# Graph layers on one core: SyncE copies the rows of 48 gather columns, GpSimd gathers 48 columns fewer

## The chip, the cores and the metric

The kernel runs on one core of a Trainium2 chip. The metric is the device time of one execution in microseconds (us). Engines are named as in the profile: PE (TensorE), DVE (VectorE), ACT (ScalarE), POOL (GpSimd), SP (SyncE). A name with a q behind it (SPq, DVEq) is the sequencer of that engine: what it issues or signals, not what it computes.

## What is computed

Four graph layers run one after the other over 6,250 nodes with 128 features and 206,250 directed edges, given as two lists, src and dst; dst is sorted. Between them stand a layer norm, a ReLU and a residual sum. Cut to what matters here:

```
h = relu(layernorm(x))
# layer 0: attention over src, sum over dst
scores = sum(query * key);  alpha = softmax of the edges with the same src
out = segment_sum(msg * alpha * count, dst);  two dense layers with batch norm
# layer 1: softmax over dst, 8 heads, with a bias from the edge features
agg = segment_sum(softmax(q[dst] . k[src] + edge @ We) * v[src], dst);  agg @ Wo
# layer 2: softmax over dst, 4 heads
out = segment_sum(softmax(leaky(e_src[src] + e_dst[dst])) * h[src], dst)
# layer 3: weighted sum over dst
agg = segment_sum(edge_weight * x[src], dst);  two dense layers, leaky relu
```

All weights, the features and the row numbers come in as float32 and int32; the output is [6250, 128] float32.

## The kernel before, in words

The edges stand in 128 partitions of T = 1612 each. A layer over the edges is a *pass*. There are five: PB goes by source (the softmax of layer 0), and PA, P1, P2 and P3 go by destination (layers 0, 1, 2, 3). A pass takes its 1612 columns in 124 halves of K = 13 columns; two halves (b = 0 and 1, each with buffers of its own) are a pair, so that a pass has 62 pairs. What one half asks of each engine:

- **POOL** (`pass_pool`, L1369 to L1383) waits for `free{b}` and issues 13 indirect DMAs (L1382). One gathers a column: for each of 128 partitions the row of a node table that the row number in `ix_s` names. Rows are 264 floats wide in PA (table `qm0`), 256 in P1 (`kv1`), 132 in P2 (`h2`), 128 in P3 (`x3`).
- **DVE** (`pass_dve`) waits for `rows{b}`, multiplies the gathered rows by the rows of the other end (L1458), reduces (L1462), does the small softmax steps, lays the next half's near rows by a scan (`hold_rows`, L1430), weights (L1517, L1521 or L1513), frees the buffer (`leave`) and scans the half (L1528).
- **ACT** (`pass_act`) takes its steps in a fixed order, half by half: the start of the next near rows (L1557, L1559), the exponentials (L1600, L1603, L1563), the copy of near rows from `rows_d` (`near_rows_act`, L1546), and then, once the half is scanned, the carried column (L1621) and the rows of state for the store (L1622, L1624). Then it signals `laid{b}`.
- **SP** (`pass_sp`, L1661) has two DMAs per half, in P1 three: the load of near rows for the pair that follows (`near_load`, L1659), in P1 the edge bias (`bias_load`, L1654), and the store of the half's state (`pass_store`, L1650), which waits for `laid{b}`.

The order of SP is written out by hand in `two` and has no loop at run time. Its core:

```
for b in range(2):
    if not last and q.near is not None:
        sp.wait_ge(*q.on("made", i * 6 + (3 * b + 1)))
        near_load(sp, q, i + 1, b)
    ...
    pass_store(sp, q, i, b)
```

So the near load that a half needs is issued by SP behind the store of the half before it, and ACT cannot reach the state rows of a half (L1621, L1622) before it has copied the near rows (L1546). P3 has no near rows: there SP has only its store.

Of the kernel before, what the change touches and what calls it, by code (L numbers as in the profile page):

```python
# [19 lines left out]
I32 = mybir.dt.int32  # L20
# [6 lines left out]
P = 128  # L27
# [7 lines left out]
T = 1612  # L35
EP = P * T
K = 13
IT = T // K
assert EP >= E and T % (2 * K) == 0
PADN = 6271  # L40
# [55 lines left out]
def graph_layers_kernel(nc, A, out):  # L96
    with ExitStack() as ctx:
        def sb(name, shape, dt=F32):
            return ctx.enter_context(nc.sbuf_tensor(name, shape, dt))
# [18 lines left out]
        def dram(name, shape, dt=F32):  # L118
            return nc.dram_tensor(name, shape, dt).ap()
# [12 lines left out]
        ident = sb("ident", [P, P])  # L132
# [30 lines left out]
        head_i = [sb(f"head_i{o}", [P, 1], I32) for o in range(2)]  # L163
        patch_i = [sb(f"patch_i{o}", [P, 1], I32) for o in range(2)]
        head = sb("head", [P, D])

        bias2 = [sb(f"bias2_{o}", [P, P]) for o in range(2)]
        contT = [sb(f"contT{o}", [P, P]) for o in range(2)]
# [128 lines left out]
        psrow_src = [stat[:, :, :, :].rearrange("p j a h -> p (j a h)")[:, b * K * 12:(b + 1) * K * 12] for b in range(2)]  # L297


        keys_dram = dram("keys_in", [2, P, C])  # L300
        sorted_dram = dram("keys_sorted", [2, P * C])
        pay_dram = dram("payload", [EP, PW])
# [6 lines left out]
        h2_t = dram("h2", [NN * P, D + 4])  # L309
        ed2_t = dram("ed2", [NN * P, 4])  # L310
        x3_t = dram("x3", [NN * P, D])
        keyrow_t = [dram(f"keyrow{o}", [P, T], I16) for o in range(2)]

        qxb_t = dram("start_rows_by_src", [EP + NPAD, D])
# [5 lines left out]
        class Pass:  # L320
# [12 lines left out]

            def own(self, what):
                return S(f"{self.name}_{what}")

            def total(self, what):

# [22 lines left out]
        P2 = Pass("p2", H2, 32, True, h2_t, ed2_t, edx_t, 136)  # L361
        P3 = Pass("p3", 1, D, False, x3_t, None, None, D)
        passes = [PB, PA, P1, P2, P3]
        for q in passes:
            q.bv, q.abig, q.st, q.psrow, q.zt, q.prod = bv, abig, st, psrow, zt, prod
# [998 lines left out]
        def gathered_rows(q):  # L1364

            return rows_3 if q is P3 else rows_s

        def pass_pool(g_, q):
            wd_s = q.tabs.shape[1]  # L1369
            to = gathered_rows(q)  # L1370
            for nm in q.needs:
                g_.wait_ge(S(nm[0]), nm[1])
            if q.near is not None:
                g_.indirect_dma_start(head[:, 0:q.HF], None, q.tabd, bass.IndirectOffsetOnAxis(ap=head_i[q.o][:, 0:1], axis=0)).then_inc(q.s("head_in"), 16)
            with g_.Fori(0, IT // 2) as i:
                for b in range(2):
                    g_.wait_ge(*q.on(f"free{b}", i + 1))
                    if q is P1:
                        g_.wait_ge(q.own(f"next{b}"), i + 1)
                    g_.sem_inc(S("pool_go"), 1)  # L1380
                    for k in range(K):
                        g_.indirect_dma_start(to[b][:, k, 0:wd_s], None, q.tabs, bass.IndirectOffsetOnAxis(ap=ix_s[b][:, k:k + 1], axis=0))\  # L1382
                          .then_inc(q.own(f"rows{b}"), 16)  # L1383

        def heads(t, q):
            return t[:, 0:q.H, :]
# [22 lines left out]
        def pass_dve(v, q):  # L1409
# [22 lines left out]
            def half(i, b, last):  # L1432
# [225 lines left out]
        def near_load(sp, q, i, b):  # L1658
            sp.dma_start(rows_d[b][:, :, :].rearrange("p t w -> p (t w)")[:, 0:K * q.HF],  # L1659
                         q.near[0:EP, :].rearrange("(p t) w -> p (t w)", t=T)[:, bass.ds(i * (2 * K * q.HF) + b * K * q.HF, K * q.HF)]).then_inc(q.s(f"near_in{b}"), 16)  # L1660

        def pass_sp(sp, q):
            for b in range(2):
                sp.sem_inc(q.s(f"sent{b}"), 16)
            if q.near is not None:
                for nm in q.started:
                    sp.wait_ge(S(nm[0]), nm[1])
            for b in range(2):
                if q.near is not None:
                    near_load(sp, q, 0, b)  # L1670
                if q is P1:
                    bias_load(sp, 0, b)

            def two(i, last):
                if q is PB:
                    zeros_chunk_sp(sp, i)
                for b in range(2):
                    if not last and q.near is not None:
                        sp.wait_ge(*q.on("made", i * 6 + (3 * b + 1)))
                        near_load(sp, q, i + 1, b)  # L1680
                    if not last and q is P1:
                        sp.wait_ge(S(f"bias_used{b}"), i + 1)
                        bias_load(sp, i + 1, b)
                    if q is PB and not b and i + 2 < NPAY:
                        payload_in(sp, i + 2)
                    if q is PB and b and i:
                        payload_out(sp, i - 1)
                    pass_store(sp, q, i, b)
                if q is PB and last:
                    payload_out(sp, i)  # L1690

            if q is PB:
                payload_in(sp, 0)
                payload_in(sp, 1)
            peeled = 2 if q is PB else 1
            for i in range(IT // 2 - peeled):
                two(i, False)
            for i in range(IT // 2 - peeled, IT // 2):
                two(i, i == IT // 2 - 1)
# [476 lines left out]
        @block.vector  # L2176
        def _(v):
            padding_dve(v)
            keys_dve(v)
            sort_dve(v, 0)  # L2180
            with v.If(unsorted(v) > 0):
                sort_dve(v, 1)
                again_dve(v)
            src_dve(v)
            pass_dve(v, PB)
            carry_dve(v, PB)
            bias_dve(v, b2_0)
# [5 lines left out]
            v.sem_inc(S("edges_ready"), 1)  # L2193
            pass_dve(v, PA)
# [12 lines left out]
            end3_dve(v)  # L2207

        @block.scalar
        def _(act):  # L2210
            norm0_act(act)
            weights3_act(act)
            dst_act(act, 0)
            proj0_sort_act(act)
            with act.If(unsorted(act) > 0):
                for lp in range(1, LOGP + 1):
                    sort_act(act, 1, lp)
                again_act(act)
# [4 lines left out]
            carry_act(act, PB)  # L2223
            pass_act(act, PA)
# [12 lines left out]
        @block.tensor  # L2237
        def _(pe):
            flag_pe(pe)
            weights3_pe(pe)  # L2240
            dst_pe(pe, 0)
            proj0_sort_pe(pe)
            with pe.If(unsorted(pe) > 0):
                for lp in range(1, LOGP + 1):
                    sort_pe(pe, 1, lp)
                dst_pe(pe, 1)
            src_pe(pe)
            payload_pe(pe)
            carry_pe(pe, PB)
            carry_pe(pe, PA)  # L2250
# [32 lines left out]
```

## Time and profile before

| | |
|---|---|
| median of 3 runs | 11,406.7 us (11,404.31 to 11,411.17) |
| profiled execution, its own time | 11,410.4 us |
| its span, first to last instruction | 11,408.5 us |
| busy: POOL, DVE, ACT, PE | 8,190.2, 7,216.0, 5,413.3, 956.1 us |
| chain that ended last | POOL 61%, issue 24%, DVE 7%, DMA 4% |

The passes take most of the span: PB from 644 to 2,660 us, PA from 2,798 to 4,836, P1 from 5,010 to 7,026, P2 from 7,183 to 9,199, P3 from 9,297 to 11,313. Between them stand the dense parts and the patches. The busy time of POOL is that of its indirect DMAs, one after the other; "issue" in the chain is the time between two of them in which POOL waited for nothing that the profile shows. A row of SPq is an issue: how long SP's sequencer was taken up by one DMA. When the bytes land is given apart, as "us to landing", counted from the issue.

### The profile page before, as it was taken

What the parts mean: (1) busy time and instruction counts of PE and PEld (TensorE: products, weight loads), DVE (VectorE), ACT (ScalarE), POOL (GpSimd) and SP (SyncE); (2) the same over time, 40 slices, a digit from 0 to 9 for tenths busy, and PEclk for the clock granted to TensorE, in tenths of its full rate; (3) what the DMA queues carried; (4) which work ended last, traced back from release to release, by engine and by line L of the source; (5) the groups of instructions that cost most, each with busy time, mean ns of one, the idle gap of its engine ahead of it and who ended that gap; (6) DMA issues with size and microseconds to landing.
All of it is one profiled execution on the core that took longest, in us unless ns stands there. A gap on an engine that the chain in (4) does not pass through costs nothing.

```text
span 11408.5 us, 38369 instructions
## 1 busy us (share of the span) xinstructions
PE 956.1 (8%) x3312; PEld 677.7 (6%) x3312; DVE 7216.0 (63%) x6971; ACT 5413.3 (47%) x6326; POOL 8190.2 (72%) x8632
## 2 busy tenths in 40 slices
PE   4122222221000000030000001100000000000001
PEld 3111111110000000010000000000000000000001
DVE  8845555553888888869999997454444543333334
ACT  6244444442666666546766765333333333333332
POOL 2177777777777777667777776777777767777776
PEclk8555565555555555565555555555555555555555
DMA  8756666663666666546666665333333333333333
GB/s 307 275 193 204 202 206 200 204 202 109 215 211 216 210 216 211 198 148 224 223 222 226 220 226 160 96 110 113 110 113 111 112 96 103 107 103 106 106 104 97
DMA packets 792030, 1943.01 MB, mean 170 GB/s; under 512 B 214034, under 2 KB 425962, under 8 KB 791369
## 3 DMA queue, kind: packets, MB, share of 16 engines
q1 hardware_dynamic: 459776, 1126.04, 28.0%
q0 software_dynamic: 331904, 814.65, 24.9%
q14 instruction: 178, 1.45, 0.0%
q8 instruction: 28, 0.46, 0.0%
q10 hardware_dynamic: 144, 0.41, 0.0%
HBM read 1201.70 MB, written 738.73 MB: 170 GB/s over the span
## 4 chain that ended last, share of the span: by engine, by line
POOL 61%; issue 24%; DVE 7%; DMA 4%; ACT 2%; PE 1%; POOLq 0%; SPq 0%; DVEq 0%; ACTq 0%
POOL region L1382 58%; DMA region<-x,ix_s 2%; DVE psR L1513 2%; POOL work L1808 1%; DVE region L656 1%; DVE region L657 1%; DVE psB L1430 1%; DVE work L1528 1%; DVE psR L1521 0%; ACT work L1622 0%; POOL start_rows_by_dst L1136 0%; POOL start_ed L972 0%; DMA region<-h,ix_s 0%; POOL start_rows_by_src L1131 0%; PE psR L759 0%
## 5 line engine op out<-in xcount | busy, mean ns | idle before, releaser
L1528 DVE TENSOR_TENSOR_SCAN work<-work,psR 128x1792 f32<-128x1792 f32 (+2 forms) x496 | 1971.3, 3974 | 92.5 <-DVE ix_s L1449 56.5
L1382 POOL DMA_INDIRECT region<-x,ix_s x1612 | 1521.2, 944 | 502.3 <-issue 460.7
L1382 POOL DMA_INDIRECT region<-qm,ix_s x1612 | 1524.0, 945 | 492.6 <-issue 490.1
L1382 POOL DMA_INDIRECT region<-kv,ix_s x1612 | 1524.1, 945 | 491.0 <-issue 484.3
L1382 POOL DMA_INDIRECT region<-k,ix_s x1612 | 1521.5, 944 | 491.2 <-issue 490.9
L1382 POOL DMA_INDIRECT region<-h,ix_s x1612 | 1521.4, 944 | 491.2 <-issue 488.8
L1546 ACT COPY work<-region 128x1664 f32<-128x1664 f32 (+1 forms) x496 | 1162.2, 2343 | 1307.2 <-DMA region<-start_rows_by_dst 775.4
L1430 DVE TENSOR_TENSOR_SCAN psB<-psB,work 128x1792 f32<-128x1792 f32 (+1 forms) x496 | 1485.1, 2994 | 397.8 <-ACT psB L1559 350.8
L1622 ACT COPY work<-work 128x1664 f32<-128x1664 f32 (+2 forms) x496 | 1539.2, 3103 | 0.0
L1621 ACT COPY psR<-work 128x128 f32<-128x128 f32 (+2 forms) x496 | 189.3, 382 | 2463.9 <-DVEq L1529 2463.9
L1458 DVE TENSOR_TENSOR work<-region,psB 128x1664 f32<-128x1664 f32 x372 | 702.1, 1887 | 808.9 <-DMA region<-k,ix_s 528.2
L1513 DVE TENSOR_TENSOR psR<-region,psB 128x1664 f32<-128x1664 f32 x124 | 235.1, 1896 | 1244.9 <-DMA region<-x,ix_s 1244.9
L1559 ACT ACTIVATE psB<-restart 128x1792 f32<-128x1792 bf16 (+1 forms) x496 | 647.4, 1305 | 15.6
L1521 DVE TENSOR_TENSOR psR<-region,psR 128x1664 f32<-128x1664 f32 x248 | 467.0, 1883 | 212.5 <-ACT work L1600 212.5
L1476 DVE TENSOR_TENSOR s_max<-region,psB 128x52 f32<-128x52 f32 x124 | 30.4, 245 | 743.1 <-DMA region<-h,ix_s 743.1
L1462 DVE TENSOR_REDUCE psR<-work 128x52 f32<-128x1664 f32 (+1 forms) x248 | 469.9, 1895 | 8.6
L1600 ACT ACTIVATE work<-dd 128x56 f32<-128x56 f32 (+2 forms) x372 | 463.0, 1245 | 0.0
L1563 ACT ACTIVATE work<-restart 128x1792 f32<-128x1792 bf16 x248 | 417.8, 1685 | 0.3
L1281 PE MATMUL psR<-work,we_wide 128*128 128x384 f32 x620 | 327.9, 705 | 870.4 <-ACT work L1303 870.4
L1770 PE MATMUL psR<-cst,contT 128*128 128x128 f32 x4 | 1.6, 501 | 4261.0 <-DVEq L1731 4261.0
L1773 PE MATMUL psB<-work,ones 128*128 128x512 f32 x6 | 5.9, 1114 | 4057.7 <-DVEq L1709 4057.7
L1557 ACT COPY work<-psB 128x128 f32<-128x128 f32 (+1 forms) x492 | 156.9, 319 | 382.2 <-DVE s_max L1476 317.5
(339 smaller groups left out, 5050.9 us busy)
## 6 DMA issues: line engine op xcount, KB each, us to landing
region<-start_rows_by_dst SPq DMA_DIRECT2D x248, 832.0 KB, 6.8
state_p<-work SPq DMA_DIRECT2D x124, 936.0 KB, 4.9
state_p<-work SPq DMA_DIRECT2D x124, 884.0 KB, 3.8
region<-start_rows_by_src SPq DMA_DIRECT2D x124, 832.0 KB, 9.9
start_rows_by_dst<-zero_t SPq DMA_DIRECT2D x62, 1664.0 KB, 7.7
state_pA<-work SPq DMA_DIRECT2D x124, 832.0 KB, 4.9
state_p<-work SPq DMA_DIRECT2D x124, 832.0 KB, 3.5
start_rows_by_src<-zero_t SPq DMA_DIRECT2D x1, 59904.0 KB, 163.6
```

What stands on the lines that cost most here:

```text
L1382: g_.indirect_dma_start(to[b][:, k, 0:wd_s], None, q.tabs, bass.IndirectOffsetOnAxis(ap=ix_s[b][:, k:k + 1], axis=0))\
L1430: nc.vector.tensor_tensor_scan(near_ps[:, 0:m], near_ps[:, 0:m], q.zt[:, 0:m], 0.0, ALU.mult, ALU.add).then_inc(q.s("held"), 1)
L1458: nc.vector.tensor_tensor(q.prod, rs[:, :, 0:D], hv[:, :, 1:K + 1].rearrange("p f t -> p t f"), ALU.mult).then_inc(q.s("dotted"), 1)
L1462: c.did(nc.vector.tensor_reduce(s.rearrange("p h t -> p t h"), q.prod.rearrange("p t (h d) -> p t h d", h=H), AX.X, ALU.add))
L1513: c.did(nc.vector.tensor_tensor(bvv[:, :, 1:K + 1].rearrange("p f t -> p t f"), rs[:, :, 0:D], w.unsqueeze(2).to_broadcast([P, K, D]), ALU ...
L1521: c.did(nc.vector.tensor_tensor(bvh[:, :, 0:dh, 1:K + 1].rearrange("p h j t -> p t h j"), rs[:, :, off:off + D].rearrange("p t (h j) -> p ...
L1528: c.do(nc.vector.tensor_tensor_scan(q.st[:, 0:F * (K + 1)], decay_at(q, b)[:, 0:F * (K + 1)], summed[:, 0:F * (K + 1)], 0.0, ALU.mult, ALU ...
L1546: nc.scalar.copy(f_by_t(q.zt, q.HF)[:, :, 1:K + 1].rearrange("p f t -> p t f"), rows_d[b][:, :, :].rearrange("p t w -> p (t w)")[:, 0:K * ...
L1559: nc.scalar.activation(f_by_t(near_ps, q.HF), restart[q.o][:, bass.ds(n, 1), :].to_broadcast([P, q.HF, K + 1]), ACT.Exp).then_inc(q.s("mad ...
L1563: return nc.scalar.activation(f_by_t(decay_at(q, b), q.F), restart[q.o][:, bass.ds(n, 1), :].to_broadcast([P, q.F, K + 1]), ACT.Exp)
L1600: nc.scalar.activation(f_by_t(decay_at(q, b), F).rearrange("p (h j) t -> p h j t", h=H), heads(dd, q).unsqueeze(2).to_broadcast([P, H, dh ...
L1622: ins = nc.scalar.copy(pr[:, :, 0:F], stv[:, :, 1:K + 1].rearrange("p f t -> p t f"))
```

## The change

In each of the four passes by destination (PA, P1, P2, P3), column 12 of half b = 1 is no longer gathered by POOL in one pair out of five: pairs 6, 11, 16, ... 61. These are 12 columns in a pass, 48 in all, one column in every ten halves. Their row numbers are the same in the four passes. They are brought once, ahead of PA: DVE copies the 12 columns of numbers (`numbers_dve`), PE turns them (`numbers_pe`), ACT copies them (`numbers_act`), and SP writes them to DRAM (`numbers_sp`). SP then waits for what the pass needs (its tables) before it starts on the pairs.

In pairs 0 to 59 of a pass, SP loads 25 or 26 of these numbers into its registers (`numbers_of`, one load instruction) and copies, for each, one row of the table to a DRAM buffer (`row_ahead`): 128 rows over five pairs, 25.6 per pair. These stand ahead of the near load of their half. Six pairs on, one DMA brings the 128 rows of the column into its place among the gathered rows (`column_in_sp`), and DVE waits for it too.

```
         def pass_sp(sp, q):
...
+            if q is AHEAD[0]:
+                numbers_sp(sp)
+            if q.ahead:
+                for nm in q.needs:
+                    sp.wait_ge(S(nm[0]), nm[1])
+
             def two(i, last):
                 if q is PB:
                     zeros_chunk_sp(sp, i)
+                j = i // PAIRS_AHEAD
+                fetch = q.ahead and j < COLS_AHEAD
+                if fetch:
+                    a, z = part_of(i)
+                    numbers = numbers_of(sp, j, a, z)
                 for b in range(2):
+                    if brought(q, i, 1) and not b:
+                        column_in_sp(sp, q, columns_ahead(i) - 1)
+                    if fetch:
+                        mid = (a + z) // 2
+                        for r in (range(a, mid), range(mid, z))[b]:
+                            row_ahead(sp, q, j, r, numbers[r - a])
                     if not last and q.near is not None:
                         sp.wait_ge(*q.on("made", i * 6 + (3 * b + 1)))
                         near_load(sp, q, i + 1, b)
```

The new functions that it calls:

```
+        def row_ahead(sp, q, j, r, number):
+
+            wd = q.tabs.shape[1]
+            sp.dma_start(ahead_t[j, r:r + 1, 0:wd], q.tabs[bass.ds(number, 1), :]).then_inc(S(f"row_ahead{column_number(q, j) % 2}"), 16)
...
+        def column_in_sp(sp, q, j):
+
+            wd = q.tabs.shape[1]
+            c = column_number(q, j)
+            sp.wait_ge(S(f"row_ahead{c % 2}"), (c // 2 + 1) * 16 * P)
+            sp.wait_ge(*q.on("free1", FIRST_AHEAD + j * PAIRS_AHEAD + 1))
+            sp.dma_start(gathered_rows(q)[1][:, K - 1, 0:wd], ahead_t[j, :, 0:wd]).then_inc(S("column_in"), 16)
```

On POOL (`pass_pool`) a half with such a column issues 12 gathers instead of 13, and on DVE (`pass_dve`) its first wait changes:

```
-                v.wait_ge(q.own(f"rows{b}"), i * (16 * K) + 16 * K)
+                v.wait_ge(*q.rows(b, gathered(q, i, b)))
+                if brought(q, i, b):
+                    v.wait_ge(S("column_in"), 16 * (column_number(q, columns_ahead(i) - 1) + 1))
```

**How instructions move on SP, PA, one half (b = 1 of the first pair).** Before, the near load stands right behind the store of the half ahead of it:

```order
L1659 DMA region<-start_rows_by_dst 128x1664 [waits pass_made]
L1650 DMA state_pA<-work 128x1664 [waits pass_laid0]
L1659 DMA region<-start_rows_by_dst 128x1664 [waits pass_made]
L1650 DMA state_pA<-work 128x1664 [waits pass_laid1]
L1659 DMA region<-start_rows_by_dst 128x1664 [waits pass_made]
```

In the changed kernel L1698 is the store, L1707 the near load, L1738 the load of numbers, and an ISA with a DMA at L1734 is one row copy (its address is worked out from the register, then the copy is issued). The same place starts so:

```order
L1698 DMA state_pA<-work 128x1664 [waits pass_laid0]
L1734 ISA
L1734 DMA rows_ahead<-qm 12x22
L1734 ISA
L1734 DMA rows_ahead<-qm 12x22
```

and ends so, with 13 such couples between store and near load:

```order
L1734 ISA
L1734 DMA rows_ahead<-qm 12x22
L1707 DMA region<-start_rows_by_dst 128x1664 [waits pass_made]
L1698 DMA state_pA<-work 128x1664 [waits pass_laid1]
L1738 TENSOR_LOAD numbers_ahead
```

Between a store and the near load that followed it at once there are now 12 or 13 row copies and, in every second half, the load of numbers too.

**On POOL, PA, the last pair of the changed loop's body of five.** Before, each half of the loop's body reads "one gather with a wait, then x12". Now the fifth half b = 1 has one less:

```order
L1406 DMA region<-qm,ix_s 128x264 [waits pass_free0]
L1406 DMA region<-qm,ix_s 128x264 x12
L1406 DMA region<-qm,ix_s 128x264 [waits pass_free1]
L1406 DMA region<-qm,ix_s 128x264 x11
```

Here L1406 is the gather that was L1382; nothing else moved on POOL.

## Rows read from the trace of the kernel before

**Rows 1.** The page: busy time of two engines, and the chain that ended last.

```profile
DVE  8845555553888888869999997454444543333334
POOL 2177777777777777667777776777777767777776
...
POOL 61%; issue 24%; DVE 7%; DMA 4%; ACT 2%; PE 1%; POOLq 0%; SPq 0%; DVEq 0%; ACTq 0%
```

**Rows 2.** Groups of instructions, line L1382 (busy us, mean ns, idle before us and releasers).

```profile
L1382 POOL DMA_INDIRECT region<-kv,ix_s x1612 | 1524.1, 945 | 491.0 <-issue 484.3 <-DVEq L1447 6.7
L1382 POOL DMA_INDIRECT region<-x,ix_s x1612 | 1521.2, 944 | 502.3 <-issue 460.7 <-DVEq L1451 30.2 <-DVE ix_s L1425 11.4
```

**Rows 3.** Timelines of SP and ACT in one half of PA (start, duration).

```profile
4008.47 0.32 SPq L1650 DMA_DIRECT2D state_pA<-work  x1
4008.83 0.43 SPq L1659 DMA_DIRECT2D region<-start_rows_by_dst  x1
4015.37 3.04 ACT L1546 COPY work<-region 128x1664 f32<-128x1664 f32 x1 [2.92 <-DMA region<-start_rows_by_dst]
4020.91 0.38 ACT L1621 COPY psR<-work 128x128 f32<-128x128 f32 x1 [2.49 <-DVEq L1529]
4024.33 0.32 SPq L1650 DMA_DIRECT2D state_pA<-work  x1
```

**Rows 4.** The same of one half of P1.

```profile
6201.97 0.32 SPq L1650 DMA_DIRECT2D state_p<-work  x1
6202.33 0.43 SPq L1659 DMA_DIRECT2D region<-start_rows_by_dst  x1
6209.81 3.04 ACT L1546 COPY work<-region 128x1664 f32<-128x1664 f32 x1 [3.39 <-DMA region<-start_rows_by_dst]
6214.18 0.17 ACT L1620 COPY psR<-m_ext 128x8 f32<-128x8 f32 x1 [1.32 <-DVEq L1529]
6218.19 0.32 SPq L1650 DMA_DIRECT2D state_p<-work  x1
```

**Rows 5.** The same of one half of P2.

```profile
8500.95 0.32 SPq L1650 DMA_DIRECT2D state_p<-work  x1
8501.32 0.43 SPq L1659 DMA_DIRECT2D region<-start_ed  x1
8511.71 0.39 ACT L1621 COPY psR<-work 128x132 f32<-128x132 f32 x1 [6.08 <-DVEq L1529]
8515.39 0.32 SPq L1650 DMA_DIRECT2D state_p<-work  x1
```

**Rows 6.** The same of one half of P3, which has no near load.

```profile
10523.74 0.38 ACT L1621 COPY psR<-work 128x128 f32<-128x128 f32 x1 [10.97 <-DVEq L1529]
```

**Rows 7.** The page, DMA issues: count, KB each, us from issue to landing.

```profile
region<-start_rows_by_dst SPq DMA_DIRECT2D x248, 832.0 KB, 6.8
state_pA<-work SPq DMA_DIRECT2D x124, 832.0 KB, 4.9
...
region<-start_ed SPq DMA_DIRECT2D x124, 26.0 KB, 3.6
```

**Rows 8.** Single lines on SP (duration ns min/median/max).

```profile
L587 SPq TENSOR_LOAD <-flag_i x4: 287/480/904, 490.2 to 4835.2; - x4
L587 SPq FUSED_REGOPS  x4: 154/158/192, 490.8 to 4835.6; - x4
L538 SPq DMA_DIRECT2D state_pA<-ctz x1: 252/252/252, 41.7 to 41.7; - x1
L494 SPq DMA_DIRECT2D we_wide<-in_L_gnn_We_dram x2: 532/564/597, 34.9 to 35.4; - x2
L494 SPq DMA_DIRECT2D be_col<-in_L_gnn_be_dram x1: 600/600/600, 36.1 to 36.1; - x1
L494 SPq DMA_DIRECT2D w3raw<-in_L_gnn_W_dram x2: 432/432/432, 39.0 to 40.4; - x2
```

More of the change, by code:

```diff
@@ L297, in graph_layers_kernel @@
         psrow_src = [stat[:, :, :, :].rearrange("p j a h -> p (j a h)")[:, b * K * 12:(b + 1) * K * 12] for b in range(2)]
+        PAIRS_AHEAD = 5
+        COLS_AHEAD = (IT // 2 - 2) // PAIRS_AHEAD
+        FIRST_AHEAD = PAIRS_AHEAD + 1
+        COL_AHEAD = FIRST_AHEAD * 2 * K + 2 * K - 1
+        assert 2 + PAIRS_AHEAD * COLS_AHEAD == IT // 2
         keys_dram = dram("keys_in", [2, P, C])
@@ L335, in own, with gathers, rows @@
                 return S(f"{self.name}_{what}")
+            def gathers(self, b):
+                return K * (IT // 2) - (COLS_AHEAD if self.ahead and b else 0)
+            def rows(self, b, value):
+                i = passes.index(self)
+                return S(f"rows{b}_{i % 3}"), value + sum(16 * q.gathers(b) for q in passes[i % 3:i:3])
             def total(self, what):
@@ L363, in graph_layers_kernel @@
         passes = [PB, PA, P1, P2, P3]
+        AHEAD = [PA, P1, P2, P3]
         for q in passes:
+            q.ahead = q in AHEAD
+            q.ahead_before = AHEAD.index(q) if q.ahead else 0
             q.bv, q.abig, q.st, q.psrow, q.zt, q.prod = bv, abig, st, psrow, zt, prod
@@ L1374, in pass_pool, with pair @@
                 g_.indirect_dma_start(head[:, 0:q.HF], None, q.tabd, bass.IndirectOffsetOnAxis(ap=head_i[q.o][:, 0:1], axis=0)).then_inc(q.s("head_in"), 16)
-            with g_.Fori(0, IT // 2) as i:
+            def pair(i, short):
                 for b in range(2):
@@ L1380, in pass_pool, with columns_ahead, brought, gathered @@
                     g_.sem_inc(S("pool_go"), 1)
-                    for k in range(K):
+                    for k in range(K - (short and b)):
                         g_.indirect_dma_start(to[b][:, k, 0:wd_s], None, q.tabs, bass.IndirectOffsetOnAxis(ap=ix_s[b][:, k:k + 1], axis=0))\
-                          .then_inc(q.own(f"rows{b}"), 16)
+                          .then_inc(q.rows(b, 0)[0], 16)
+            if q.ahead:
+                pair(0, False)
+                pair(1, False)
+                with g_.Fori(0, COLS_AHEAD) as j:
+                    for u in range(PAIRS_AHEAD):
+                        pair(j * PAIRS_AHEAD + (u + 2), u == PAIRS_AHEAD - 1)
+            else:
+                with g_.Fori(0, IT // 2) as i:
+                    pair(i, False)
+        def columns_ahead(i):
+            return max(0, (i - 1) // PAIRS_AHEAD)
+        def brought(q, i, b):
+            return q.ahead and b and i >= FIRST_AHEAD and (i - FIRST_AHEAD) % PAIRS_AHEAD == 0
+        def gathered(q, i, b):
+            return 16 * (K * (i + 1) - (columns_ahead(i) if q.ahead and b else 0))
         def heads(t, q):
@@ L1660, in near_load, with numbers_dve, numbers_pe, numbers_act @@
                          q.near[0:EP, :].rearrange("(p t) w -> p (t w)", t=T)[:, bass.ds(i * (2 * K * q.HF) + b * K * q.HF, K * q.HF)]).then_inc(q.s(f"near_in{b}"), 16)
+        def numbers_dve(v):
+            nc.vector.tensor_copy(numbers_f[:, :], oth_i[1][:, COL_AHEAD:T:2 * K * PAIRS_AHEAD]).then_inc(S("numbers"), 1)
+        def numbers_pe(pe):
+            pe.wait_ge(S("numbers"), 1)
+            nc.tensor.transpose(numbers_ps[0:COLS_AHEAD, :], numbers_f[:, :], ident[:, :]).then_inc(S("numbers"), 1)
+        def numbers_act(act):
+            act.wait_ge(S("numbers"), 2)
+            nc.scalar.copy(numbers_i[:, :], numbers_ps[0:COLS_AHEAD, :]).then_inc(S("numbers"), 1)
+        def numbers_sp(sp):
+            sp.wait_ge(S("numbers"), 3)
+            sp.dma_start(numbers_t, numbers_i[:, :]).then_inc(S("numbers"), 16)
+            sp.wait_ge(S("numbers"), 19)
+        def column_number(q, j):
+            return q.ahead_before * COLS_AHEAD + j
+        def row_ahead(sp, q, j, r, number):
+            wd = q.tabs.shape[1]
+            sp.dma_start(ahead_t[j, r:r + 1, 0:wd], q.tabs[bass.ds(number, 1), :]).then_inc(S(f"row_ahead{column_number(q, j) % 2}"), 16)
+        def numbers_of(sp, j, a, z):
+            return nc.values_load_multi_w_load_instructions(numbers_t[j:j + 1, a:z], engines=(mybir.EngineType.SP,), min_val=0, max_val=PADN,
+                                                            skip_runtime_bounds_check_because="a row number is the number of a node, at most PADN")[1]
+        def column_in_sp(sp, q, j):
[4 more added lines that the diff above has]
+            sp.dma_start(gathered_rows(q)[1][:, K - 1, 0:wd], ahead_t[j, :, 0:wd]).then_inc(S("column_in"), 16)
+        def part_of(i):
+            u = i % PAIRS_AHEAD
+            return P * u // PAIRS_AHEAD, P * (u + 1) // PAIRS_AHEAD
         def pass_sp(sp, q):
@@ L1672, in pass_sp @@
                     bias_load(sp, 0, b)
+            if q is AHEAD[0]:
+                numbers_sp(sp)
+            if q.ahead:
+                for nm in q.needs:
+                    sp.wait_ge(S(nm[0]), nm[1])
             def two(i, last):
```

8 lines of the change are left out of this document (added).

## The prediction
> **What bounds the kernel now.** I read the page first, for who is busy and what the chain of waits ends on. POOL is busy seven tenths in almost every slice, and POOL with its issue gaps is 85% of the chain [rows 1]. Then the gathers by pass: 1,612 of them, 945 ns each, with 0.30 us of issue gap between them and next to no wait for another engine; (1,524.1 + 491.0) / 1,612 = 1.25 us a column, 16.25 us a half of 13 columns and 32.5 us a pair, in all five passes [rows 2]. So POOL sets the pace, and a gather removed is worth at most 1.25 us.
>
> Then I asked who comes next, since a pass has three more engines with a fixed round per half. The timelines of PA and P1 show a second loop that is nearly as long. It runs through SP: ACT lays a half's state, SP issues the store and 0.36 us behind it the near load, the near rows land, ACT copies them (L1546), and only behind that, in ACT's own order, come L1621 and L1622, which lay the next half's state. The reader is to see in [rows 3, 4] that ACT stands idle for the near load (2.92 and 3.39 us), and that the slack of this loop is the wait of ACT that follows, for the scan: 2.49 us in PA, 1.32 us in P1. In P2 the near load is small and the slack is 6.08 us [rows 5]. P3 has no near load; its ACT waits 10.97 us a half for DVE [rows 6].
>
> **The gain.** 48 gathers go: 48 x 1.25 = 60 us, if POOL stays the bound. In a half without them DVE is not the limit in PA, P2 and P3 [rows 1]; in P1 it is nearly full, and perhaps 10 of the 60 stay there. So 50 to 60 us, 0.5% of the time.
>
> **What SP now issues.** Per pair, 25.6 row copies and one load of 25 or 26 numbers, in 60 of 62 pairs of each of the four passes: 6,144 copies, 240 loads. All stand between a store and the near load behind it, which is inside the loop above. Their price:
>
> - The address: one FUSED_REGOPS, 0.158 us [rows 8].
> - The copy's issue. SP's static copies take from 0.252 us (one row) to 0.432 us (128 rows). The built program marks nearly all of them as prepared ahead; two kinds in the weights' loads without that mark take 0.532 to 0.600 us [rows 8]. A copy whose address comes out of a register can't be prepared, so I take 0.56 us, the nearest rows. The ends are 0.25 us and, for what no row shows of register addresses, 0.87 us (0.56 plus twice the address step).
> - The step from one SP instruction to the next, 0.04 us (4008.47 + 0.32 to 4008.83) [rows 3], twice.
>
> That is 0.80 us a row (0.48 to 1.1) and 25.6 x 0.80 = 20.5 us a pair.
> - The load of numbers. A load of a single number takes 0.287 to 0.904 us, median 0.48 [rows 8]. For 25 the ends are 0.5 us (all at the price of one) and 25 x 0.287 = 7.2 us; nothing says which is nearer, and I take the middle, 3.8 us.
>
> Together S = 24.3 us a pair. The Trainium skill, page "Runtime: NRT & Kernel Launch", section "Instruction fetch mechanics", puts such a load at about 200 ns per register even in bulk; by that it would be an estimated 5.1 us a pair and the sum below 1.3 x 180 = 234 us more. No run here shows it yet.
>
> **The loop with S in it.** Per half, without waits:
>
> - PA: store to near load 0.36, copy 3.04, L1621 to the next store 3.42 (4020.91 to 4024.33), and the landing. Now 6.54 us pass from the issue (4008.83) until ACT has the rows (4015.37) [rows 3]. But behind a dozen row copies the near load no longer starts beside the 832 KB store; the store itself lands in 4.9 us with the load on its heels, against 6.8 for the load [rows 7]. I take 4.9 for the landing and keep 6.5 as the upper end. A half is 6.82 + 4.9 = 11.7 us, a pair 23.4 + 24.3 = 47.7 us against 32.5: 15.2 us x 60 pairs = **+912**.
> - P1: 0.36 + 3.04 + 4.01 (6214.18 to 6218.19) + 4.9 = 12.3 us; 7.48 us is the upper end of the landing [rows 4]. A pair is 24.6 + 24.3 = 48.9, so 16.4 x 60 = **+984**.
> - P2: 0.37 (8500.95 to 8501.32) + 3.6 for the landing [rows 7] + 0.26 for its short copy + 3.68 (8511.71 to 8515.39) [rows 5] = 7.9 us; a pair 15.8 + 24.3 = 40.1: 7.6 x 60 = **+456**. In P2 the slack of 6.08 us a half is eaten as well.
> - P3: SP needs 2 x 0.32 + 24.3 = 25 us of 32.5 a pair, and nothing is behind it but stores with two halves of room. It keeps its gain: **-15**.
>
> Sum: 912 + 984 + 456 - 15 = +2,337. Where the loop is the bound the removed gathers give nothing. The sum is against the profiled execution, 11,410.4 us (span 11,408.5 and 1.9 around it), 4 us above the median; on the median it gives about 13,750.
>
> **Small edits.** The copy of the numbers on DVE, the turn on PE, the copy on ACT and the write happen once, between PB and PA, by rows of 0.2 to 0.5 us and one DMA that lands like a small load, 3.6 us: under 10 us. SP's new wait for the tables delays only pair 0. The DMA that brings a column is one issue of about 0.43 us in 48 pairs, 20 us at most, and it is issued a half before DVE asks. What the copies move is 6,144 rows of about 1 KB, 6 MB of 1,943: no load for the DMA engines. On DVE the added wait finds its data there.
>
> **The rivals.** (a) *Faster*: the copies hide. The deciding point is what SP adds per half against the slack: 1.32 us in P1, 2.49 in PA, and up to 1.6 to 2.6 us more if the landing shortens. With 13 copies that is 0.2 to 0.35 us a row, all told. Then POOL stays the bound and the time is 11,406.7 - 55 = 11,350. For it speaks that SP has two short issues a half and idles 15 of 16 us; against it, that this idleness lies behind the store's wait and the copies stand in front of the near load, and that 0.158 + 0.252 + 0.08 = 0.49 us is the least the rows allow. The skill's page "DMA: Bandwidth & Descriptors", section "Issuing engines are not separate DMA queues", calls the sequencer's time to initiate a DMA usually small beside the DMA itself; by that rule this case would hold. [...]
>
> (b) *Slower, but little*: issues as short as prepared ones (0.49 us a row) and the numbers at the price of one. S = 25.6 x 0.49 + 0.5 = 13.0; PA 36.4 and P1 37.6 us a pair, +234 and +306, P2 28.8 us and hidden: 11,406.7 + 540 - 30 = 11,920.
>
> (c) *Much slower*: a register address costs more, 1.1 us a row, and the numbers 7.2 us. S = 35.4; pairs of 58.8, 60.0, 51.2 and 36.0 us: +1,578, +1,650, +1,122, +210, so about 15,970.
>
> (d) The column comes late and DVE waits for it. The rows are copied at least a pair before the DMA that collects them, so it would take a landing of over 16 us; it would add at most some us in 48 halves. It changes no sum.
>
> **How the numbers follow.** Two kernels differ measurably here from about 0.2%, 23 us. The forecast (slower through the near-load loop, S between 16 and 31 us) has 0.74, (b) and what lies below 16 us 0.11, (c) and beyond 0.10, (a) 0.04, no change 0.01. S = 16 gives 39.4, 40.6 and 31.8 us a pair, +414, +486 and nothing in P2, so about 12,280. S = 31 gives 54.4, 55.6, 46.8: +1,314, +1,386, +858, about 14,950. The range is these two, 12,280 to 14,950. Chances: faster 0.04, same 0.01, slower 0.95.
>
> **What the profile of the changed kernel would show.** The couples at L1734 at 0.80 us on SP, near loads issued 10 us and more behind their store; ACT idle before L1546 for the near load by some 10 us a half in PA and P1, and no wait any more at L1621 and L1620; POOL waiting at its first gather of a half, for DVE; PB and P3 as long as before, P3 shorter by 15 us; P1 the longest pass, P2 less stretched than PA. Near-load landings below 6.8 us. I would be wrong if ACT's wait at L1621 stays, if POOL still has only issue gaps in PA, or if the copies overlap their issue.

## The result and the profile after

The changed kernel takes 14,658.5 us (median of 4 runs, 14,653.0 to 14,667.3) against 11,408.8 us of the kernel before on the same chip: 1.285 times the time, 95% interval 1.2827 to 1.2872, or +3,250 us. The forecast was 13,750 with a range of 12,280 to 14,950: the right way, with a size 910 us short.

The page, in the lines that answer to [rows 1]:

```profile
DVE  8555555445444454555556556633333333433333
...
POOL 1477777644444444454444444465555555677776
...
SPq 34%; POOL 20%; issue 17%; DMA 13%; ACT 10%; DVE 5%; PE 1%; ACTq 0%; POOLq 0%; DVEq 0%
SPq L1734 23%; POOL region L1406 18%; SPq L1738 10%; DMA region<-start_rows_by_dst 8%; ACT work L1670 8%; DMA region<-start_ed 2%; DMA region<-x,ix_s 2%; DVE psR L1561 1%; POOL work L1917 1%; DVE region L679 1%; ACT psR L1669 1%; DVE region L680 1%; SPq L1698 1%; ACT work L1672 0%; DVE work L1576 0%
```

The slices are 367 us long. From the ninth on, just behind the start of PA, POOL is busy four to six tenths, and seven again only in the last ones, which are P3. SP's sequencer had 0% of the chain before; now it has 34%, and it names the row copies (L1734, 23%) and the loads of numbers (L1738, 10%). The gathers (source L1406, was L1382: ns min/median/max, first and last start) date the passes:

```profile
L1406 POOL DMA_INDIRECT region<-qm,ix_s x1600: 940/947/959, 2804.3 to 6206.8; - x178
L1406 POOL DMA_INDIRECT region<-kv,ix_s x1600: 940/947/1040, 6405.4 to 9524.2; - x178
L1406 POOL DMA_INDIRECT region<-h,ix_s x1600: 938/945/984, 9688.6 to 12467.9; - x178
L1406 POOL DMA_INDIRECT region<-x,ix_s x1600: 940/945/961, 12568.6 to 14566.0; - x178
```

A gather costs what it cost [rows 2]. First to last gather of a pass, in us (first and last starts in the traces), on chips on which the kernel before takes 11,407 to 11,409 us:

| | PA | P1 | P2 | P3 | the whole kernel |
|---|---|---|---|---|---|
| before | 2,014 | 2,014 | 2,011 | 2,011 | 11,409 |
| after | 3,403 | 3,119 | 2,779 | 1,997 | 14,659 |
| near load first (e1) | 2,303 | 2,248 | 2,097 | 1,996 | 12,008 |
| gathers back (e2) | 3,362 | 3,086 | 2,740 | 2,013 | 14,565 |
| numbers aligned (e3) | 3,115 | 2,793 | 2,457 | 1,996 | 13,726 |
| fixed rows, no numbers (e4) | 2,674 | 2,561 | 2,027 | 1,996 | 12,621 |
| near load first, aligned (e11) | 2,067 | 2,015 | 1,996 | 1,996 | 11,430 |

After minus before is +1,389, +1,105, +768 and -14, together 3,248 of the 3,250 us.

One half of PA, from a store to the next (timelines of SP and ACT after; L1698 store, L1734 copies, L1707 near load, L1594 near copy, L1669 and L1670 state rows), against [rows 3]:

```profile
3846.95 0.32 SPq L1698 DMA_DIRECT2D state_pA<-work  x1
3847.47 12.01 SPq L1734 DMA_DIRECT2D rows_ahead<-qm  x13
3859.52 0.50 SPq L1707 DMA_DIRECT2D region<-start_rows_by_dst  x1
3870.42 0.32 SPq L1698 DMA_DIRECT2D state_pA<-work  x1
```

```profile
3864.19 3.02 ACT L1594 COPY work<-region 128x1664 f32<-128x1664 f32 x1 [13.37 <-DMA region<-start_rows_by_dst]
3867.03 0.36 ACT L1669 COPY psR<-work 128x128 f32<-128x128 f32 x1
3867.32 3.04 ACT L1670 COPY work<-work 128x1664 f32<-128x1664 f32 x1
```

13 copies take 12.0 us; the near load goes out 12.6 us behind its store instead of 0.36, its rows are there 4.7 us later, and ACT runs straight through to the next store: 23.5 us instead of 15.9, with no wait left at L1669. The half after that holds a load of numbers too. Over the passes, two lines of the page say who waits: ACT for the near rows, 15.8 us a half in PA and P1 (3,849.6 us in 244 waits), and POOL in PA for DVE to free a buffer.

```profile
L1594 ACT COPY work<-region 128x1664 f32<-128x1664 f32 (+1 forms) x496 | 1159.5, 2338 | 6266.3 <-DMA region<-start_rows_by_dst 3849.6
L1406 POOL DMA_INDIRECT region<-qm,ix_s x1600 | 1514.0, 946 | 1891.5 <-DVEq L1497 1438.4
```

What SP pays (a copy of a row is cut into parts: 12 of 22 or 11 floats in PA and P2, 16 of 16 or 8 in P1 and P3; source views of L1734, L1738 and L1707, ns min/median/max; "us to landing" of the page), against [rows 7, 8]:

```profile
L1734 SPq FUSED_REGOPS  x6144: 37/37/48, 2810.7 to 14511.2; - x199
L1734 SPq MOVE rows_ahead<-qm x1536: 29/38/45, 2810.8 to 6155.3; - x192
L1734 SPq DMA_DIRECT2D rows_ahead<-qm x1536: 701/729/1325, 2810.9 to 6155.3; - x192
...
L1734 SPq DMA_DIRECT2D rows_ahead<-kv x1536: 492/492/1392, 6414.0 to 9472.8; - x192
...
L1734 SPq DMA_DIRECT2D rows_ahead<-h x1536: 701/724/1160, 9692.2 to 12425.0; - x192
```

```profile
L1738 SPq TENSOR_LOAD <-numbers_ahead x240: 2950/10690/12007, 2807.3 to 14482.5; - x120
```

```profile
region<-start_rows_by_dst SPq DMA_DIRECT2D x248, 832.0 KB, 5.0
...
region<-start_ed SPq DMA_DIRECT2D x124, 26.0 KB, 2.3
```

Within a half, copies start 0.924 us apart in PA (median; mean 0.944), 0.675 in P1 (mean 0.718), 0.918 in P2 (0.942). A load of 25 or 26 numbers takes 10.7 us in the median and 8.2 in the mean of PA, P1 and P2. With these the forecast's own loop gives, per pair: PA 2 x (6.82 + 5.0) + 24.2 + 8.2 = 56.0 us, P1 2 x (7.41 + 5.0) + 18.4 + 8.2 = 51.4, P2 2 x (0.37 + 2.3 + 0.26 + 3.68) + 24.1 + 8.1 = 45.4. Measured, as 32.5 + growth / 60: 55.6, 50.9 and 45.3 us.

### The profile page after: what moved, and what is told of

It reads as the page before. It is cut to its first block, busy times and chain, and to the rows that moved or that the text cites. A ratio compares the mean times of both kernels' runs of the same rounds, so it can differ in the third digit from the quotient of the medians.

```text
span 14665.2 us, 56702 instructions
## 1 busy us (share of the span) xinstructions
PE 956.2 (7%) x3313; PEld 678.2 (5%) x3313; DVE 7210.5 (49%) x6972; ACT 5339.6 (36%) x6327; POOL 8152.4 (56%) x8584
## 4 chain that ended last, share of the span: by engine, by line
SPq 34%; POOL 20%; issue 17%; DMA 13%; ACT 10%; DVE 5%; PE 1%; ACTq 0%; POOLq 0%; DVEq 0%
SPq L1734 23%; POOL region L1406 18%; SPq L1738 10%; DMA region<-start_rows_by_dst 8%; ACT work L1670 8%; DMA region<-start_ed 2%; DMA region<-x,ix_s 2%; DVE psR L1561 1%; POOL work L1917 1%; DVE region L679 1%; ACT psR L1669 1%; DVE region L680 1%; SPq L1698 1%; ACT work L1672 0%; DVE work L1576 0%
## 5 line engine op out<-in xcount | busy, mean ns | idle before, releaser
L1594 ACT COPY work<-region 128x1664 f32<-128x1664 f32 (+1 forms) x496 | 1159.5, 2338 | 6266.3 <-DMA region<-start_rows_by_dst 3849.6
L1406 POOL DMA_INDIRECT region<-qm,ix_s x1600 | 1514.0, 946 | 1891.5 <-DVEq L1497 1438.4
L1406 POOL DMA_INDIRECT region<-kv,ix_s x1600 | 1514.4, 946 | 1605.6 <-DVEq L1493 1154.2
L1406 POOL DMA_INDIRECT region<-h,ix_s x1600 | 1511.2, 945 | 1269.3 <-DVEq L1497 818.1
L1576 DVE TENSOR_TENSOR_SCAN work<-work,psR 128x1792 f32<-128x1792 f32 (+2 forms) x496 | 1971.3, 3974 | 92.0 <-DVE ix_s L1495 55.6
L1406 POOL DMA_INDIRECT region<-k,ix_s x1612 | 1522.8, 945 | 491.1 <-issue 490.8
L1406 POOL DMA_INDIRECT region<-x,ix_s x1600 | 1511.3, 945 | 498.7 <-issue 456.4
L1670 ACT COPY work<-work 128x1664 f32<-128x1664 f32 (+2 forms) x496 | 1536.9, 3099 | 0.0
L1669 ACT COPY psR<-work 128x128 f32<-128x128 f32 (+2 forms) x496 | 185.9, 375 | 1408.7 <-DVEq L1577 1389.2
L1542 DVE TENSOR_TENSOR_SCAN m_ext<-rst,psR 128x112 f32<-128x112 f32 (+1 forms) x248 | 81.5, 329 | 429.2 <-ACT work L1672 427.6
```

Of the source, the lines that this page charges most:

```text
L1576: c.do(nc.vector.tensor_tensor_scan(q.st[:, 0:F * (K + 1)], decay_at(q, b)[:, 0:F * (K + 1)], summed[:, 0:F * (K + 1)], 0.0, ALU.mult, ALU ...
L1594: nc.scalar.copy(f_by_t(q.zt, q.HF)[:, :, 1:K + 1].rearrange("p f t -> p t f"), rows_d[b][:, :, :].rearrange("p t w -> p (t w)")[:, 0:K * ...
L1670: ins = nc.scalar.copy(pr[:, :, 0:F], stv[:, :, 1:K + 1].rearrange("p f t -> p t f"))
```

## The experiments

Theory N: the copies and loads of numbers lengthen the loop store, near load, near copy, state rows, because they stand between store and near load. Its rivals are named in each expectation. e1 to e4 ran on one chip (kernel before 11,407.7), one execution each.

**e1: the near load first.** In `two`, the near load and the bias load move ahead of the rest (the same lines go from their old places):

```
                 for b in range(2):
+                    if not last and q.near is not None:
+                        sp.wait_ge(*q.on("made", i * 6 + (3 * b + 1)))
+                        near_load(sp, q, i + 1, b)
+                    if not last and q is P1:
+                        sp.wait_ge(S(f"bias_used{b}"), i + 1)
+                        bias_load(sp, i + 1, b)
                     if brought(q, i, 1) and not b:
                         column_in_sp(sp, q, columns_ahead(i) - 1)
                     if fetch:
+                        if not b:
+                            numbers = numbers_of(sp, j, a, z)
```

Expected:

> Only the order on SP changes: in each half the near load (and in P1 the bias load) is issued ahead of the load of numbers and of the row copies, so that the copies stand before the store instead of before the near load. Theory N (the copies lengthen the loop store, near load, near copy, state rows): SP's time no longer adds to that loop. What stays is SP's own time in the halves that hold a slow load of numbers (11.0 us, three of five) and 12 or 13 copies: 23 us in PA and P2, 20 in P1, against 16.25; such a pair should take about 37, 35 and 37 us, the others 32.5, so PA +170, P1 +105, P2 +150 us and P3 -15: 11,800 us, between 11,600 and 12,000. Theory D (the many small copies hold up the DMA engines or the landing of the loads, wherever SP issues them) expects the time of the changed kernel, 14,660 within 200. Theory W (SP's total work is what counts, not its place) expects at least 60 pairs x (33.3 - 32.5) in PA only if SP never idles, and otherwise no relief: over 13,500.

Measured 12,008 us: 2,650 of the 3,250 us are gone with the place alone, the work being the same to the last copy (1,536 in each pass, 0.729, 0.492 and 0.724 us). D (the copies hurt wherever they stand) and W (SP's total work counts, not its place) fall as accounts of the 3,250 us. The number lies 8 us above N's range, for PA, P1 and P2 keep +290, +234 and +86 where 170, 105 and 150 were expected. One reason shows in the trace: beside near load and store a load of numbers takes longer.

```profile
L1738 SPq TENSOR_LOAD <-numbers_ahead x240: 2957/10338/15066, 2805.7 to 11825.4; - x120
```

The mean is 10.7 us in PA and P1 (8.2 after), 7.9 in P2, which has the small near load.

**e2: POOL gathers all columns again.** The copies stay and nothing reads them; DVE's count of gathers is set back and its added wait goes too.

```
-                    for k in range(K - (short and b)):
+                    for k in range(K):
...
-                        column_in_sp(sp, q, columns_ahead(i) - 1)
+                        c = column_number(q, columns_ahead(i) - 1)
+                        sp.wait_ge(S(f"row_ahead{c % 2}"), (c // 2 + 1) * 16 * P)
```

> POOL gathers all 1612 columns again, DVE's added wait and the DMA that brings a column are gone, SP still loads the numbers and copies all rows (and still waits for them where the column would have been brought). Theory N: POOL is not the bound in PA, P1 and P2, so giving back its 36 gathers there costs nothing; only P3 grows by 12 x 1.25 = 15 us: 14,660 to 14,680. Rival G (part of the loss is the wait of DVE for the column, or the shorter POOL half starting its gathers beside the near load) expects a time below 14,600.

Measured 14,565 us. P3 grew by 16 us as expected; PA, P1 and P2 shrank by 41, 32 and 40, though 36 gathers came back. So the gathers buy nothing there, which is N's point; but the total is outside N's numbers and inside G's. Of these 113 us, 57 are in the loads of numbers (1,417 us in the three passes against 1,474; their median fell by 0.5 us), and about 13 in the 36 DMAs that bring a column (0.33 us each and the step to the next). The trace speaks against G's causes for the other 43: outside its load of numbers, a pair without such a column is shorter as well, by 0.3 us in the mean, and a pair with one by 0.6 us, of which its DMA is 0.36. So no wait of DVE for the column shows. What made all pairs 0.3 us shorter stays open.

**e3: numbers that start at multiples of 16 bytes.**

```
-            return P * u // PAIRS_AHEAD, P * (u + 1) // PAIRS_AHEAD
+            return P * u // PAIRS_AHEAD // 4 * 4, P * (u + 1) // PAIRS_AHEAD // 4 * 4
```

> The 128 numbers of a column are cut at multiples of 4 (0, 24, 48, 76, 100, 128) instead of 0, 25, 51, 76, 102, so that each load of numbers starts at a multiple of 16 bytes. In the changed kernel the loads that start at 0 and at 304 bytes take 3.5 to 4.0 us and those that start at 100, 204 and 408 bytes 10.8 to 11.2. Theory A (the start of the read decides): all loads take 3.4 to 4.2 us, the mean falls from 8.1 to 3.8, and 180 pairs of PA, P1 and P2 lose 4.3 us each: 14,660 - 770 = 13,890, within 60. Rival C (what decides is what else is under way at that pair, such as the DMA that brings a column or the age of the table): the loads of the second, third and fifth part stay near 11 us and the time near 14,660.

Measured 13,726 us, -933. A is right, C falls:

```profile
L1738 SPq TENSOR_LOAD <-numbers_ahead x240: 2474/2962/6360, 2806.5 to 13541.8; - x120
```

The size was missed because the loads fell below 3.5 us: mean 3.1, so (8.2 - 3.1) x 180 = 918. By the part of the column: 24 numbers 2.8 us, 28 numbers 3.3; in the changed kernel 25 and 26 numbers from an aligned start 3.4 and 3.9, from the others 10.7 to 11.2. These are medians over all passes. They fit 0.47 us for each 16 bytes taken whole (6 x 0.47 = 2.8, 7 x 0.47 = 3.3, and one or two numbers more at 0.43 each make 3.3 and 3.7) and, from the other starts, 0.43 us for each single number (25 x 0.43 = 10.7). It is a fit to these lengths and starts; how SP reads them no run shows.

**e4: fixed rows and no numbers.** The 48 brought columns hold other rows than the reference's.

```
-                    numbers = numbers_of(sp, j, a, z)
...
-                            row_ahead(sp, q, j, r, numbers[r - a])
+                            row_ahead(sp, q, j, r, 48 * r)
```

> Each copied row is taken from a fixed row of the table (row 48 r) instead of the one whose number stands in a register, and the loads of numbers are left out; the 48 brought columns then hold other rows than the reference's. As many copies of the same size, at the same place on SP. Theory R (the register address makes the copy dear: no preparation ahead, 0.49 to 0.72 us plus 0.11 for its two address steps): a copy takes 0.28 to 0.34 us, 0.04 between two, S = 25.6 x 0.36 = 9 us a pair; with 23.4, 24.6 and 15.8 us for the rest of the loop PA is 32.6 and P1 33.8 a pair, P2 and P3 hidden: 11,410 + 80 - 45 = 11,450, up to 11,700. Rival Q (what is dear is a DRAM to DRAM copy cut into 12 or 16 parts, whatever its address): 0.49 and 0.72 us stay, S = 14 to 20, and the time is 12,000 to 12,700.

```profile
L1734 SPq DMA_DIRECT2D rows_ahead<-qm x1536: 676/677/1838, 2805.5 to 5424.6; - x192
L1734 SPq DMA_DIRECT2D rows_ahead<-kv x1536: 467/589/1620, 5674.7 to 8183.1; - x192
L1734 SPq DMA_DIRECT2D rows_ahead<-h x1536: 676/677/1539, 8398.1 to 10381.6; - x192
```

Measured 12,621 us. R falls and Q's number holds: without a register the copy still takes 0.68 us in 12 parts and 0.59 in 16 (medians). The register isn't what makes it dear: with it the copy takes 0.05 us more in 12 parts and 0.10 us less in 16, and FUSED_REGOPS, MOVE and two more steps of 0.04 us stand beside it, so that copies start 0.20 us further apart in PA (0.924 against 0.720) and 0.04 in P1 (0.675 against 0.632). The reason that the prediction gave for its 0.56 us (a register address can't be prepared) was wrong, though the number lies between those measured, 0.49 and 0.73. Whether it is the copy from DRAM to DRAM or its cut into parts that makes it dearer than the 0.25 us of [rows 8], this run doesn't tell apart.

**The joint repairs.** e5 (e1 and e3 together), e6 (the same, one column in twelve halves), e7 (rows padded to 272 and 144 floats, one column in eight halves) and e8 (loads of numbers, but one copy a pair) ran on a second chip, e9 and e10 (e5's and e7's kernels again) on a third, e11 (e5's kernel) on a fourth, e12 on a fifth. On the second, third and fifth the kernel before itself took 12,792, 12,775 and 12,786 us, so those runs stand by themselves below.

> Both repairs together: near load (and bias load) ahead of numbers and copies, and loads of numbers that start at multiples of 16 bytes. One column in ten halves as before. SP's time in a half with a load of numbers is now about 0.9 + 3.0 to 4.4 + 12.2 x 0.92 = 15.2 to 16.6 us in PA and P2 against a half of 16.25, and 13 in P1. Theory N: the loop through the near load is as it was, POOL is the bound again, and 48 x 1.25 = 60 us come back, less what P1's DVE and ACT keep (10 to 15): 11,350 to 11,380. Rival W (SP is full in PA and P2 whatever the order): PA and P2 stay above 32.5 us a pair and the time is over 11,450.

> The kernel of e5_first_aligned a third time, after the two runs before fell on chips where the kernel before itself takes 12,780 us. If the kernel before takes about 11,408 here, theory N expects 11,350 to 11,380 (60 us of gathers back, less 10 to 15 that P1's DVE and ACT keep) and rival W (SP full in PA and P2) over 11,450. If it takes 12,780 again, the run says only that such a chip punishes SP's copies each time: 15,000 to 15,150.

e11, with the kernel before at 11,407.2 (13 runs): 11,430.5 us (10 runs), ratio 1.0019, interval 1.001 to 1.0029, 23 us slower. That is outside both theories' numbers, 50 us above N's and 20 below W's, and by pass each is right in part. Of 3,250 us all but 23 are undone by the place and the cut of the numbers. By pass it is PA +53, P1 +2, P2 -15, P3 -15. P2 and P3 have their 15 us. P1 has none of its gain: its ACT still waits for the near load, 3.4 us a half (411.3 / 120) as before, and its DVE is busy 1,860 of 2,020 us; which of the two holds it, no run shows. PA is a case of W:

```profile
3822.12 0.32 SPq L1698 DMA_DIRECT2D state_pA<-work  x1
3822.49 0.42 SPq L1707 DMA_DIRECT2D region<-start_rows_by_dst  x1
3829.28 11.32 SPq L1734 DMA_DIRECT2D rows_ahead<-qm  x12
3840.64 0.51 SPq L1698 DMA_DIRECT2D state_pA<-work  x1
3841.19 0.43 SPq L1707 DMA_DIRECT2D region<-start_rows_by_dst  x1
```

Between 3822.91 and 3829.28 SP loads numbers (6.3 us in the mean of PA, beside near load and store), then come 12 copies, and SP reaches the next store after 18.5 us where a half has 16.25.

**Chips on which the kernel before takes 12,780 us.** Expected:

> The same with one column in twelve halves (10 in a pass, 40 in all), which leaves SP two copies fewer in each half. Theory N: 40 x 1.25 = 50 us less 8 to 12 for P1: 11,360 to 11,380, and SP with room in every pass, so that PA, P2 and P3 all shrink by 12.5 us. Rival W: if the run before is over 11,450, this one lies below it.

> Near load first, aligned loads, and the tables of PA and P2 padded from 264 to 272 and from 132 to 144 floats a row (zeros; gathered and copied with the rest), so that a row copy is cut into 16 parts instead of 12 in all passes; with that one column in eight halves (15 in a pass, 60 in all), 32 copies a pair. Theory K (the number of parts sets the issue: 12 parts 0.70 to 0.73 us, 16 parts 0.49): all copies take 0.49 us, SP needs 32 x 0.675 + 4 + 2 = 28 us a pair of 32.5, and 75 us less 15 to 20 for P1 come off: 11,345 to 11,360. Rival L (what costs in PA and P2 is the length or the start of the row, not the cut): the copies stay at 0.7 us, SP needs 36 us a pair in PA and P2, and the time is over 11,600.

> The changed kernel's loads of numbers at their place ahead of the near load, but one row copy a pair instead of 25 or 26, and POOL gathers all columns. Theory N: a pair of PA with an 11 us load is 13.7 + 11.5 + 11.1 + 0.9 = 37.2 us, one with a 3.5 us load stays at 32.5, so 2.8 us on average and +170 in PA; P1 the same way 38.8 and 32.5, +227; P2 is at 28 us and hidden, P3 too: 11,800, between 11,700 and 11,900. Rival (the two costs are not of one loop: the loads overlap with waits of SP and only the copies hurt): 11,410 to 11,500.

> The kernel of e5_first_aligned again, because that run and its companions fell on a chip on which the kernel before itself took 12,792 us. On a chip where the kernel before takes about 11,408, theory N expects 11,350 to 11,380 and rival W over 11,450, as said there.

> The kernel of e7_wide4 again, for the same reason. Its copies took 0.492 us in all four passes there, which bears theory K out. With the kernel before at 11,408, SP needs 28 us a pair of 32.5 and 60 gathers fewer should give 11,345 to 11,360; over 11,450 if SP is full all the same.

> From the run before: P2 and P3 got their 16 us, P1 nothing, PA lost 52 us because in halves with a load of numbers (6.3 us there, beside near load and store) SP came to the store about 19 us after the last one. Here the tables of PA and P2 are padated to 272 and 144 floats a row, so that a copy is cut into 16 parts (0.49 us instead of 0.73), and a third of a pair's copies, not half, stands in the half with the load of numbers; one column in ten halves. Theory N: SP needs 0.9 + 6.3 + 8.5 x 0.675 = 13 us in that half and 0.9 + 17 x 0.675 = 12.4 in the other, under 16.25 in every pass; PA -15, P1 0, P2 -16, P3 -16: 11,350 to 11,370 where the kernel before takes 11,407. Rival V (what costs in PA is the load of numbers and the copies running beside near load and store, not SP's time): PA stays over 2,040 us, the time over 11,400.

The edit of e6 beside e5's:

```
-PAIRS_AHEAD = 5
+PAIRS_AHEAD = 6
```

That of e7, e10 and e12, beside zeros in the pads:

```
-PAIRS_AHEAD = 5
+PAIRS_AHEAD = 4
-        qm0_t = dram("qm0", [NN * P, 264])
+        qm0_t = dram("qm0", [NN * P, 272])
-        h2_t = dram("h2", [NN * P, D + 4])
+        h2_t = dram("h2", [NN * P, 144])
-        WS = 264
+        WS = 272
```

e12 has the padded tables too, but keeps `PAIRS_AHEAD = 5` and has `mid = a + (z - a) // 3` (the first half gets a third of the copies). That of e8, in the changed kernel's own order, with all columns gathered by POOL and nothing that reads the copies:

```
-                    if fetch:
-                        mid = (a + z) // 2
-                        for r in (range(a, mid), range(mid, z))[b]:
-                            row_ahead(sp, q, j, r, numbers[r - a])
+                    if fetch and b:
+                        row_ahead(sp, q, j, z - 1, numbers[z - 1 - a])
```

Measured (this, before, ratio with its 95% interval):

| | this | before | ratio |
|---|---|---|---|
| e5 | 15,016 | 12,792 | 1.175 (1.169 to 1.181) |
| e6 | 14,664 | 12,792 | 1.144 (1.137 to 1.151) |
| e7 | 14,902 | 12,792 | 1.163 (1.159 to 1.168) |
| e8 | 12,836 | 12,792 | one execution |
| e9 | 15,097 | 12,775 | 1.186 (1.180 to 1.192) |
| e10 | 15,048 | 12,775 | 1.180 (1.175 to 1.185) |
| e12 | 14,880 | 12,786 | 1.162 (1.159 to 1.166) |

The kernel that was 23 us slower on one chip is 2,224 and 2,323 us slower on these. Even PB, which no edit touches, takes 2,365 us from first to last gather in e9 (2,012 before), with the gathers' own time unchanged:

```profile
L1406 POOL DMA_INDIRECT region<-k,ix_s x1612: 940/947/988, 652.1 to 3017.1; - x180
```

and P3, where no near load waits, takes 2,673. Within a half of PA, 534 of 1,416 steps from one copy to the next are over 1.05 us in e9; in e1 it was 76. What that does is seen in P3 of e5:

```profile
13027.46 9.83 SPq L1734 DMA_DIRECT2D rows_ahead<-x  x14
13037.34 0.57 SPq L1698 DMA_DIRECT2D state_p<-work  x1
13040.65 14.36 SPq L1734 DMA_DIRECT2D rows_ahead<-x  x12
13055.02 0.69 SPq L1698 DMA_DIRECT2D state_p<-work  x1
13057.86 32.59 SPq L1734 DMA_DIRECT2D rows_ahead<-x  x12
```

14 copies take 9.8 us there, 12 others 14.4 or 32.6, and each store stands right behind the last copy. In the mean copies start 1.58 us apart in P3 and 1.45 to 1.61 in the other passes, though the medians of their own durations are those of the other chips. That is 25.6 x 1.58 = 40 us of SP a pair for the copies alone, of the 42.9 us that a pair of P3 takes (2,661 / 62). In all four passes of e5 a store goes out 0.05 us behind what stands ahead of it (median), so SP hardly waits for anything: there SP is full, and theory W holds whatever the order. Two more runs fit: e8, with one copy a pair, is 44 us slower than the kernel before, where e5 is 2,224 (its P3 takes 2,231 us), and e6, with 1,024 copies fewer than e5, is 352 us faster. What makes the gaps, no run tells. e8 is one execution, and N's +400 for it could not be tested on a chip where a half takes 18 us anyway.

Only what a copy takes can be carried over. In e7 the medians are

```profile
L1734 SPq DMA_DIRECT2D rows_ahead<-qm x1920: 1/492/1610, 3222.7 to 5933.4; - x192
...
L1734 SPq DMA_DIRECT2D rows_ahead<-h x1920: 1/492/1483, 9162.3 to 11754.9; - x192
```

0.492 us in PA and P2, where e5 on the same chip has 0.729 and 0.723 with 12 parts. Theory K, the number of parts, stands; the length falls, for these rows are longer. The padding also moves where rows start, but e4 speaks against that: row 48 r starts at a multiple of 64 bytes within either table, and none of its copies in 12 parts took less than 0.676 us. Whether e12's kernel beats the one before on a chip like e11's stays open; it never ran on one. No version that ran is faster than the kernel before.

## Why the prediction was right, and where it was short

- **The bound and the second loop: right.** The growth is in PA, P1 and P2 and nowhere else, ACT has no wait left at L1669 in the half shown, and POOL waits for DVE at its first gathers. ACT's wait for the near load is 15.8 us a half, not some 10, since SP's work is longer than forecast. e1 shows that the place in SP's order is the cause on such a chip, not the copies as such.
- **The order of the passes: half right.** P1 was forecast to grow most (984 against 912); PA did, 1,389 against 1,105, because its copies have 12 parts (0.92 us apart) and P1's 16 (0.675). I had one price, 0.80 us, for both. By itself this moved PA up by about 25.6 x 0.14 x 60 = 215 us, P2 the same, and P1 down by 130, together +300.
- **The load of numbers: too small.** I had ends of 0.5 and 7.2 us and took the middle, 3.8: it was 8.2 in the mean, above my upper end, which took the least duration of a single load as the price per number. The term is (8.2 - 3.8) x 180 = 790 us and most of the 910 that are missing. The Trainium skill's "Runtime: NRT & Kernel Launch" (section "Instruction fetch mechanics") has about 200 ns per register. The traces have 120 to 430 ns by where the read starts (2.8 us for 24 numbers in e3, 10.7 for 25 here), so the measurement decides, and the page's 5.1 us would have left some 680 of the 910 us open.
- **The landing: right for PA and P1.** 4.9 us taken, 5.0 measured, since the near load no longer runs beside the store: in e1, where it does again, ACT has the rows 6.1 and 6.4 us behind the issue in two halves of PA. For P2 the forecast kept 3.6; it fell to 2.3, which gave 2 x 1.3 x 60 = 156 us back.
- **Inside the range, in part by luck.** The range stood for 16 to 31 us of SP a pair. Measured were 24.2 + 8.2 = 32.4 in PA and 32.2 in P2, above it, and 26.6 in P1. The total stayed below 14,950 because P1's copies were cheaper than the one price and P2's landing shorter.
- **The address and the copy: right in sum, wrong in parts.** FUSED_REGOPS took 0.037 us, not 0.158; a MOVE of 0.03 us and a third step of 0.04 stood beside it. No run shows that "prepared ahead" sets the 0.56 us: in e4 a fixed address left the copy at 0.68 and 0.59.
- **The gain: right where it could be seen.** P3 -14 (forecast -15).
- **Rival (a): wrong.** It needed 0.2 to 0.35 us a row; the rows took 0.68 to 0.92. The Trainium skill's "DMA: Bandwidth & Descriptors" (section "Issuing engines are not separate DMA queues") calls the time to initiate a DMA usually small beside the DMA. The traces have no landing time for these copies, so they don't test that; they show that the 0.5 to 0.7 us of issue, 6,144 times, is what SP paid.

## What to carry to other kernels

An engine that shows hardly any busy time is still no free resource: ask what stands behind each of its waits, and put new work behind the last instruction that somebody waits for, not in front of it (e1: 2,650 of 3,250 us). Price work in the units of the engine that takes it over: 128 row copies and their numbers cost SP 120 to 160 us for one gather of 1.25 us on POOL, so this trade can win at most 0.5% (the 60 us of 48 gathers), and it needs SP nearly empty. And when a term has no row, the upper end must come from a mechanism (each number its own read at the median price would have been 12 us), not from the smallest row at hand.

## What the runs showed that I had not expected

- A load of numbers from DRAM into SP's registers took about 0.47 us for each 16 aligned bytes and 0.43 us for each single number when the start was not a multiple of 16 bytes: 24 numbers 2.8 us (e3), 25 misaligned 10.7 (after). Beside near load and store the same aligned loads took 6.3 us in the mean (e11, PA).
- A DRAM to DRAM copy of one row whose address stands in a register took 0.49 us to issue in 16 parts and 0.73 in 12, whatever its length (512 or 1,024 bytes in 16 parts; 528 or 1,056 in 12). With a fixed address it was 0.59 and 0.68 (e4).
- On three of the five chips of the experiments the kernel before took 12% more than elsewhere, and kernels with 5,120 to 7,680 copies on SP took 29% to 32% more than the kernel before takes elsewhere, for SP's instructions came with gaps that filled it (e5).
